# Doubling a split product on ScalarE instead of VectorE, and fewer semaphore waits on TensorE, in a per-sequence low-rank update

## What is computed

```python
def reference(x, itok_B_3_7, L0_cond_A, L0_cond_B):   # x (64, 64, 1024)
    B_sel = B[adapter_ids]                            # (64, 16, 1024)
    A_sel = A[adapter_ids]                            # (64, 1024, 16)
    Bx = jnp.einsum('bni,bri->bnr', x, B_sel)
    out = jnp.einsum('bnr,bor->bno', Bx, A_sel)
    return x + out * SCALING                          # SCALING = 1.0
```

## Time and profile before

| | |
|---|---|
| median of 3 runs | 95.53 us |
| profiled execution | 95.39 us, span 93.5 us |
| TensorE busy (matmul) | 81.1 us, 87% of the span |
| VectorE busy | 66.8 us, 71% |
| GpSimd busy | 65.1 us, 70% |
| ScalarE busy | 53.3 us, 57% |
| DMA | 34.82 MB, mean 372 GB/s |

### The profile page before, as it was taken

How to read it: one execution, slowest core, us unless ns; L and a number is a source line. 1 busy time by engine, 2 the same in 40 slices (tenths; PEclk the granted TensorE clock), 3 DMA queues, 4 the chain that set the end, 5 groups by cost and what they waited for, 6 DMA issues and landing times.

```text
span 93.5 us, 3679 instructions
## 1 busy us (share of the span) xinstructions
PE 81.1 (87%) x1466; PEld 62.9 (67%) x1466; DVE 66.8 (71%) x124; ACT 53.3 (57%) x139; POOL 65.1 (70%) x140
## 2 busy tenths in 40 slices
PE   3996899999999999799999799999997999933910
PEld 3996798787786868486877586877785878611400
DVE  0069541228798989597989598989794979899960
ACT  1356877986747576647667557667673667430000
POOL 6048946999897979686979497978786969360000
PEclk9999999999999999999999999999999999997555
DMA  2899999999999999999999999999999988576595
GB/s 39 291 392 413 406 410 406 408 410 417 396 406 413 405 406 405 406 399 406 410 415 410 417 422 403 417 413 410 419 408 417 413 336 329 201 291 263 217 399 242
DMA packets 10193, 34.82 MB, mean 372 GB/s; under 512 B 834, under 2 KB 1858, under 8 KB 10178
## 3 DMA queue, kind: packets, MB, share of 16 engines
q1 hardware_dynamic: 10032, 34.08, 91.4%
q10 hardware_dynamic: 146, 0.52, 1.8%
HBM read 17.83 MB, written 16.78 MB: 370 GB/s over the span
## 4 chain that ended last, share of the span: by engine, by line
PE 71%; DVE 13%; DMA 5%; issue 3%; POOL 2%; ACT 1%; POOLq 0%
PE t_bank L226 32%; PE bx_bank L239 18%; PE y_banks L259 18%; DVE x_all L368 9%; DMA x_all<-in_A 5%; PE y_banks L217 4%; DVE bx_parts L354 3%; POOL x_all L174 2%; DVE bx_parts L361 1%; ACT a_table L308 1%; ACT x_t L303 1%; DVE x_all L339 0%; POOLq L173 0%
## 5 line engine op out<-in xcount | busy, mean ns | idle before, releaser
L368 DVE TENSOR_TENSOR x_all<-y_banks,x_all 128x1024 f32<-128x1024 f32 x32 | 39.1, 1224 | 10.2 <-PE y_banks L259 9.7
L303 ACT COPY x_t<-t_bank 128x512 f32<-128x512 f32 x64 | 34.5, 590 | 20.7 <-PE t_bank L226 20.6
L166 POOL CAST a_duo<-a_table 128x512 fp32r x64 | 37.7, 634 | 4.7 <-PE y_banks L259 2.7
L226 PE MATMUL t_bank<-ident,x_all 128*128 128x128 f32 x256 | 35.2, 279 | 0.4 <-ACT x_t L303 0.4
L226 PEld LDWEIGHTS t_bank<-ident,x_all 128*128 128x128 f32 x256 | 27.4, 141 | 7.3 <-issue 5.8
L156 POOL COPY b_duo<-b_table 128x256 f32 x64 | 22.9, 403 | 8.8 <-PE bx_bank L239 8.8
L259 PE MATMUL y_banks<-a_duo,bx_parts 64*128 64x512 f32 x128 | 21.1, 439 | 4.6 <-DVE bx_parts L361 2.9
L239 PE MATMUL bx_bank<-x_t,b_duo 128*32 128x64 f32 x1024 | 21.0, 222 | 0.5 <-issue 0.5
L239 PEld LDWEIGHTS bx_bank<-x_t,b_duo 128*32 128x32 f32 x1024 | 15.8, 109 | 6.1 <-issue 5.9
L354 DVE TENSOR_TENSOR bx_parts<-bx_bank,bx_parts 32x64 fp32r<-32x64 f32 x64 | 14.1, 220 | 4.8 <-ACT bx_parts L318 3.7
L259 PEld LDWEIGHTS y_banks<-a_duo,bx_parts 64*128 64x128 f32 x128 | 10.9, 192 | 9.4 <-issue 5.0
(11 more groups left out here) (12 smaller groups left out, 10.1 us busy)
## 6 DMA issues: line engine op xcount, KB each, us to landing
out_y<-x_all SPq DMA_DIRECT2D x32, 512.0 KB, 10.9
x_all<-in_x SPq DMA_DIRECT2D x15, 1024.0 KB, 18.9
x_all<-in_x SPq DMA_DIRECT2D x2, 512.0 KB, 6.3
x_all<-in_B ACTq DMA_DIRECT2D x1, 512.0 KB, 4.5
x_all<-in_A SPq DMA_DIRECT2D x2, 256.0 KB, 5.0
id_row<-in_ids ACTq DMA_DIRECT2D x1, 0.2 KB
```

What stands on the lines that cost most here:

```text
L166: last = nc.gpsimd.tensor_copy(a_duo[duo % 2][:, k, :], a_table[:, bass.ds(adapters[k] * BANK, BANK)])
L226: last = nc.tensor.transpose(t_bank[unit % 2][:, c * P:(c + 1) * P], x_all[:, 2 * duo + tile, at:at + P], ident[:, :])
L303: nc.scalar.copy(x_t[duo % 2][:, half * HALF:(half + 1) * HALF, tile, :], t_bank[unit % 2][:, :].rearrange("p (c n) -> p c n", c=HALF)).th ...
L368: nc.vector.tensor_tensor(here, product, here, ALU.add).then_inc(y_drained, 1)
```

## The change

ScalarE gets `double_parts`. In its loop the copy for duo - 1 stands between the second and the third `copy_x` of duo + 1, and the last two stand ahead of and behind `split_high(15)`. On TensorE a unit waits for its x only where the transfer is a new one: 17 such waits stay of 64. `down` no longer waits for `rest_done`.

```diff
             def transpose_unit(duo, unit):
                 tile, half = unit // 2, unit % 2
-                pe.wait_ge(x_loaded[LOAD_OF[2 * duo + tile]], 16)
+                if unit == 0 or duo == 0 and half == 0:
+                    pe.wait_ge(x_loaded[LOAD_OF[2 * duo + tile]], 16)
                 pe.wait_ge(t_copied, B_UNITS + UNITS * duo + unit - 1)
...
             def down(duo, first, end):
                 if first == 0:
                     pe.wait_ge(b_gathered, duo + 1)
-                    if duo >= 2:
-                        pe.wait_ge(rest_done, duo - 1)
...
+            def double_parts(duo):
+                act.wait_ge(rest_done, duo + 1)
+                nc.scalar.copy(own_tokens(duo, K_UP, 2 * K_UP),
+                               own_tokens(duo, 0, K_UP)).then_inc(parts_done, 1)
...
             for duo in range(DUOS):
                 if duo + 1 < DUOS:
-                    for unit in range(UNITS):
-                        copy_x(duo + 1, unit)
+                    copy_x(duo + 1, 0)
+                    copy_x(duo + 1, 1)
+                if duo:
+                    double_parts(duo - 1)
+                if duo + 1 < DUOS:
+                    copy_x(duo + 1, 2)
+                    copy_x(duo + 1, 3)
                 split_high(duo)
+            double_parts(DUOS - 1)
...
-            def double_parts(duo):
-                dve.wait_ge(rest_done, duo + 1)
-                nc.vector.tensor_copy(own_tokens(duo, K_UP, 2 * K_UP),
-                                      own_tokens(duo, 0, K_UP)).then_inc(parts_done, 1)
...
             split_rest(0)
-            double_parts(0)
             for duo in range(1, DUOS):
                 add_x(duo - 1, 0)
                 split_rest(duo)
-                double_parts(duo)
                 add_x(duo - 1, 1)
```

## The result

The changed kernel takes **93.03 us** (median of 4 runs, 92.94 to 93.05) against 95.41 us for the kernel before in the same comparison (4 runs, 95.15 to 95.58): ratio 0.975, 95% interval 0.9725 to 0.9777. That is 2.4 us faster. The prediction had 94.5 and a range that ended at 93.6: right in sign, too small by more than half.

A forecast was written before the change was run, and what follows sets the result against it. TensorE was taken to be paced by its instruction supply, pieces of 256 arriving every 6.4 us. From 95.39, less 0.95 for waits and 0.07 for the tail, came 94.37, so 94.5 for the median; range 93.6 to 95.6.

The forecast's parts named there:

- The bound: TensorE's program arrives in pieces of 256 instructions every 6.4 us, against 6.12 us wanted; four stops, 2.5 us.
- Rival 1: TensorE's separate waits were free or the grid's new places give the gain back; only the tail counts, 95.45; chance 0.16.
- It stays paced: 256 instructions are now 6.22 us of work, still under 6.4: TensorE after the change still waits for its program pieces; stops shrink from 2.5 to some 1.6 us.
- the first term, the waits: 47 separate TensorE waits dropped, 179 instead of 182 instructions per duo: 0.075 us less per duo, 0.95 us taken.
- the 4.47 to 4.50 forecast: Sign of being right: mean period per duo in us, against 4.57 before.
- rival 2: All four TensorE stops vanish or each wait costs its 51 ns: 93.0, likelier half of this, 93.8; chance 0.12.
- its form of pieces just in time: Rival 2's variant: program pieces arrive just in time and all four TensorE stops vanish, 2.5 us.
- 51 ns per wait: Rival 2's other variant: each of the 47 dropped TensorE waits costs its dispatch time, 2.4 us.
- The doubling in mid-program: VectorE's 16 copies moved to ScalarE's idle gap: 0 both ways, the earlier second add_x swallowed by the pacing.
- The tail: At the end, ScalarE doubling lets VectorE's adds start earlier; last up at 86.60 instead of 86.67, 0.07 us gained.
- the slower rival: ScalarE's tail copy takes 0.59 or more instead of 0.40, up(15) 0.30 later; 95.8 with waits free; chance 0.07.
- its half form: Rival 2 with half of the recovery, 1.7 us, giving 93.8; held to be its likelier form.

The follow-up runs named there:

- the padded runs: Fulfilled waits added: six per transposing unit on the swapped-waits kernel (194 instructions per duo), 100.08 us; four per unit on the changed kernel (187), 97.49 us.
- the lightly stored ones: Only the first 128 of 1024 output columns stored: kernel with 194 instructions per duo 96.55 us (100.08 with full stores), kernel before 92.59 us.
- the padded run: Kernel before with its two waits per transposing unit swapped and six fulfilled waits more per unit, 194 instructions per duo: 100.08 us, ratio 1.048.
- 182: Kernel before with only the doubling moved to ScalarE, all TensorE waits kept: 94.91 us, ratio 0.994.
- the one with 183 instructions: Changed kernel with two fulfilled waits more per transposing unit, 183 instead of 179 instructions per duo: 94.59 us, ratio 0.995.
- the one with 194: Kernel before with swapped waits and six fulfilled waits more per transposing unit, three separate instructions more: 100.08 us, ratio 1.048.

## Why the prediction was wrong

- **The bound, right.** TensorE paced by pieces of 256 instructions, the stops on a grid, waits that cost by their number: the padded runs (about 100 forecast, 100.08; 96.5 to 98.5, 97.49) and the lightly stored ones bear it out. The packets of the kernel before end 6.2 to 7.0 us apart between 37.19 and 69.61. Rival 1, waits that are free, is out. The page "Runtime: NRT & Kernel Launch" of the Trainium skill, section "Instruction fetch mechanics", holds the crossing of pieces to be mostly hidden: the trace agrees where the DMA engines are idle (share 0.14) and disagrees where they are full.
- **"It stays paced: 256 instructions are now 6.22 us of work, still under 6.4": the step that failed.** This sized the first term, the waits, at 0.95 us and let the pacing swallow what the doubling gives in mid-program. What they measured: the waits alone 1.5 us, the doubling on top of them 0.9; together the periods gave 2.81 us, to 4.34 instead of the 4.47 to 4.50 forecast. I had taken the interval between two stops for the supply's own pace. 6.36 to 6.73 is the pace of a TensorE that stops; pieces for one that does not have to come only every 56.42 / 13 x 256 / 179 = 6.21 us, and they did, nine times. Near that balance the cost is not proportional, as the slope of 0.6 instead of 0.33 us per instruction shows. A stop goes with a late next piece: under full stores, between 20 and 70 us, the next packet starts 4.2 us in the mean after a step with a stop (3.6 to 4.7) and 3.3 after one without (2.2 to 5.0). That a queue which does not stop enters a piece ahead of the work, and so asks earlier, is only argued.
- **"Everything is recovered", rival 2 at 0.12,** was what happened, in its form of pieces just in time (2.5 us, against 2.81 measured), not in that of 51 ns per wait, which the padded run rules out.
- **The doubling in mid-program, held to be 0: wrong.** I had seen that the second `add_x` would start 0.58 earlier and called it swallowed by the pacing. It is 0.5 us alone and 0.9 with the waits, the larger of the two errors in the sum. ScalarE's side of the step was right: 0.40 us in its gap, no `copy_x` late.
- **The tail, 0.07 forecast, 0.14 measured,** right in sign and place; the slower rival (a ScalarE copy over 0.47 us) did not come, the copy took 0.405.
- **A term that was missing:** 1.0 us given back at the end, 2.7 to 3.7 us from issue to landing of the last store, by one DMA engine that runs on alone. The forecast subtracted TensorE's gain from the end one for one.
- **The range** let the place of the grid and the spread of the pieces count 0.5 us, and took rival 2 in its half form only. A full removal of the four stops had been worked out, 93.0, and left outside.

## What to carry to other kernels

Where the matmul engine stops with no semaphore to blame, count its instructions between the stops: multiples of 256 say that its program comes late, the packets of the instruction queue show it by when they end, and then every separate wait counts as an instruction and the data's DMA traffic as its competitor. Near the balance of supply and demand do not scale the loss with the count; forecast between "all stops gone" and "proportional", and hold both in the range. An engine off the bound can still matter if it makes the bound engine pause for a few hundredths of a microsecond, and a gain of the engines is worth at the end only what the last stores let through.

## What was not expected of the hardware

- The cliff: with the doubling on ScalarE and 179 instructions per duo no stop in nine pieces, with 182 and 183 three each, with 187 a stop at nearly every piece; 4.46 us for 8 instructions per duo.
- A kernel at this balance spreads more: the kernel before ran from 94.3 to 95.8 us over these comparisons, in all but two of its runs, and the one with 183 instructions from 93.9 to 95.2, in all but one, while the changed one kept within 92.94 to 93.05 and the one with 194 within 99.83 to 100.09.
- Which of two waits rides on a matmul and which becomes an instruction of its own follows from the order in which they are written; for the time it mattered little here (95.17 against 95.2 to 95.5).
